# Three of the second scan's input products through ScalarE and TensorE, and all first weight parts at its first pair

## What is computed

```python
def step(h, inp):
    dt_t, B_t, C_t, x_t = inp
    dA = jnp.exp(dt_t[..., None] * A)
    h = dA * h + (dt_t * x_t)[..., None] * B_t[:, None, :]
    y = jnp.einsum('bdn,bn->bd', h, C_t)
    return (h, y)
...
for e in range(E):
    h = jax.nn.gelu(xf @ w1[e] + b1[e], approximate=False)
    y = h @ w2[e] + b2[e]
    out = out + combine[:, e:e + 1] * y
```

## Time and profile before

| | us |
|---|---|
| median of 3 runs | 208.72 |
| lowest and highest | 206.53, 208.76 |
| the profiled execution's time | 208.26 |
| its span, first to last instruction | 206.5 |
| TensorE busy in the span | 183.0 (89%) |
| weight loads | 151.8 (73%) |
| VectorE, ScalarE, GpSimd busy | 130.9, 122.5, 105.3 |

### The profile page before, as it was taken

How to read it: one execution, slowest core, us unless ns; L and a number is a source line. 1 busy time by engine, 2 the same in 40 slices (tenths; PEclk the granted TensorE clock), 3 DMA queues, 4 the chain that set the end, 5 groups by cost and what they waited for, 6 DMA issues and landing times. The chain is left out here.

```text
span 206.5 us, 3725 instructions
## 1 busy us (share of the span) xinstructions
PE 183.0 (89%) x1202; PEld 151.8 (73%) x1202; DVE 130.9 (63%) x312; ACT 122.5 (59%) x281; POOL 105.3 (51%) x140
## 2 busy tenths in 40 slices
PE   6899868996797389799998999999998999999993
PEld 5677744652262134478997989899998999999992
DVE  2575999999999869951373836562357573334333
ACT  2707998999543564424567646776555555455540
POOL 5510044779787795692555435544375344444400
PEclk9999999999999769999999999999999999999999
DMA  5950299997560000000000000000000000000000
GB/s 154 327 176 0 71 363 349 326 317 212 184 227 0 0 0 0 0 0 3 0 2 0 3 2 0 3 0 0 3 0 5 0 2 0 3 27 3 0 0 25
DMA packets 7233, 14.38 MB, mean 70 GB/s; under 512 B 512, under 2 KB 3112, under 8 KB 6960
## 3 DMA queue, kind: packets, MB, share of 16 engines
q1 hardware_dynamic: 7216, 14.17, 21.3%
HBM read 13.88 MB, written 0.29 MB: 69 GB/s over the span
## 5 line engine op out<-in xcount | busy, mean ns | idle before, releaser
L345 POOL TENSOR_TENSOR hc<-hs,cb 128x1024 f32<-128x1024 f32 x16 | 37.6, 2355 | 25.0 <-DMA cb<-c_rows 13.0
L905 DVE SCALAR_TENSOR_TENSOR acc<-dbx_ps,comb,acc 128x128 f32<-128x128 f32 x96 | 29.0, 345 | 33.4 <-PE dbx_ps L1184 33.0
L1156 PE MATMUL bc_ps<-x_hi,w_hi 128*128 128x256 f32 x128 | 42.3, 330 | 0.8 <-DVE dbx_ps L761 0.8
L612 ACT ACTIVATE hid<-bc_ps,par 128x256 f32<-128x256 f32 x64 | 26.8, 471 | 25.3 <-PE bc_ps L1158 25.1
L359 POOL TENSOR_TENSOR w_lo<-w1b,w_hi 128x256 fp32r<-128x256 f32 x32 | 23.5, 736 | 27.4 <-ACT w_hi L604 27.1
L771 DVE TENSOR_TENSOR_SCAN hs<-da,dbx_ps 128x1024 f32<-128x1024 f32 x16 | 36.4, 2278 | 0.1
L1158 PE MATMUL bc_ps<-x_hi,w_lo 128*128 128x256 f32 x128 | 36.0, 281 | 0.0
L1157 PE MATMUL bc_ps<-x_lo,w_hi 128*128 128x256 f32 x128 | 35.8, 280 | 0.0
L1184 PE MATMUL dbx_ps<-w2b,hid 128*128 128x128 f32 (+1 forms) x256 | 33.9, 276 | 0.8 <-DVE acc L905 0.8
L1184 PE MATMUL dbx_ps<-w2a,hid 128*128 128x128 f32 x256 | 34.1, 276 | 0.3 <-ACT hid L612 0.2
L359 POOL TENSOR_TENSOR w_lo<-w1a,w_hi 128x256 fp32r<-128x256 f32 x32 | 23.2, 732 | 21.6 <-ACT w_hi L604 21.6
(11 more groups left out here) (178 smaller groups left out, 233.7 us busy)
## 6 DMA issues: line engine op xcount, KB each, us to landing
w1a<-w_in SPq DMA_DIRECT2D x2, 1024.0 KB, 8.9
cb<-c_rows SPq DMA_DIRECT2D x2, 1024.0 KB, 6.1
w1b<-w_in SPq DMA_DIRECT2D x2, 1024.0 KB, 14.4
cb<-c_rows SPq DMA_DIRECT2D x2, 768.0 KB, 5.6
cb<-taps_in SPq DMA_DIRECT2D x1, 512.0 KB, 4.9
cb<-c_rows SPq DMA_DIRECT2D x2, 256.0 KB, 3.7
par<-packed_in SPq DMA_DIRECT2D x1, 473.0 KB, 3.8
x_cm<-x_in SPq DMA_DIRECT2D x2, 128.0 KB, 2.1
```

What stands on the lines that cost most here:

```text
L345: nc.gpsimd.tensor_tensor(hc[p][:], hs[p][:], cb[:, k].rearrange("p i (o t) -> p i o t", o=1).to_broadcast([128, PAIR, DC, T]), ALU.mult). ...
L612: ins = nc.scalar.activation(hid[p][:, c, :], h_ps[p][:, T * c:T * (c + 1)], ACT.Gelu, bias=par[:, bass.ds(u * UC + at, 1)])
L905: nc.vector.scalar_tensor_tensor(acc[k][:, t, :], o_ps[:, w // span % RING, 128 * t:128 * (t + 1)], comb[layer][b][:, t, bass.ds(u, 1)], a ...
L1156: nc.tensor.matmul(h_ps[p][:, T * c:T * (c + 1)], w1_hi[w][:, at], x_hi[b][:], start=True, stop=False)
```

## The change

Three pairs of batch 1's scan, m = 11, 13 and 15 (`TURNED`), no longer get their product from `spread_b` and `inputs`. Once, `turn` (TensorE, four transposes) brings `dtx` of batch 1 into token-major order in `f_ps`, and ScalarE copies it to `dtx_tok`. For each of the three pairs `token_products` (ScalarE) makes four 128x256 products with a column of `b_tok` as the scale of each partition, and `turned_product` (TensorE) turns them with eight transposes into the pair's `dbx` slot, after scan m-2 has released it. In the order of the engines: on ScalarE the copy and the products of pair 11 stand in `pair_in` of k=0, behind the decays of pairs 8 to 11 and ahead of `stage`; those of 13 behind the decays of 13 at k=2; those of 15 behind the decays of 15 at k=4, ahead of `expert_in`. On TensorE `turn` stands behind `spread_b` of pair 10, and the turned products in `pair_in` of k = 2, 4 and 6, the last one ahead of `lead`. All four `stage` steps stand at k=0, ahead of `weigh` of pair 8 on GpSimd. Counts of `b_ready` and `dbx_done` are reduced by `made`. Four scratch tiles (`dt_a`, `dt_e`, `dt_l`, `dt_q`) have one copy for both batches.

```diff
+TURNED = (NP + 3, NP + 5, NP + 7)
...
+        def made(m):
+
+            return m - sum(p < m for p in TURNED)
...
             plan += [("pair_in", 1, k)] + [(name, 0, 0) for name in before_states.get(k, [])]
-            if k in (0, 2):
-                plan += [("stage", k), ("stage", k + 1)]
+            if k == 0:
+                plan += [("stage", u) for u in range(STAGED)]
...
+            def token_products(m):
+
+                j = TURNED.index(m)
+                if j >= RING:
+                    act.wait_ge(s["dbx_pe"], j - RING + 1)
+                for i in range(PAIR):
+                    for t in range(TT):
+                        n = PAIR * (m % NP) + i
+                        ins = nc.scalar.activation(dbx_tok[j % RING][:, i, t, :], dtx_tok[:, t, :], ACT.Identity,
+                                                   scale=b_tok[:, m // NP, t, n:n + 1])
+                ins.then_inc(s["dbx_tok_ready"], 1)
+
             def pair_in(b, k):
 
                 for j in (range(AHEAD) if b and k == 0 else (k + AHEAD - 1,) if b else (k,)):
                     if j < NP:
                         decays(b, j, (j + NP * b) % AHEAD)
+                if (b, k) == (1, 0):
+                    act.wait_ge(s["turn_ps"], 1)
+                    nc.scalar.activation(dtx_tok, f_ps.rearrange("p (t d) -> p t d", t=TT), ACT.Copy).then_inc(s["turned"], 1)
+                    act.wait_ge(s["turned"], 1)
+                if b and k % 2 == 0 and NP + k + 3 in TURNED:
+                    token_products(NP + k + 3)
...
                 m = k + NP * b
-                dve.wait_ge(s["dbx_done"], m + (1 + RING))
+                if m in TURNED:
+                    dve.wait_ge(s["dbx_pe"], TURNED.index(m) + 1)
+                else:
+                    dve.wait_ge(s["dbx_done"], made(m) + (1 + RING))
...
                 m = k + NP * b + 1
-                if 1 < m < NB * NP:
+                if 1 < m < NB * NP and m not in TURNED:
                     inputs(m // NP, m % NP, m % RING)
...
+            def turn():
+
+                pe.wait_ge(s["dtx_ready"], 1)
+                for t in range(TT):
+                    for c in range(DC):
+                        ins = nc.tensor.transpose(f_ps[:, 128 * (DC * t + c):128 * (DC * t + c + 1)], dtx[1][:, c, 128 * t:128 * (t + 1)], ident[:])
+                ins.then_inc(s["turn_ps"], 1)
+
+            def turned_product(m):
+
+                pe.wait_ge(s["dbx_tok_ready"], TURNED.index(m) + 1)
+                pe.wait_ge(s["h_done"], m - 1 + RING)
+                for t in range(TT):
+                    for c in range(DC):
+                        for i in range(PAIR):
+                            ins = nc.tensor.transpose(dbx[m % RING][:, i, c, 128 * t:128 * (t + 1)],
+                                                      dbx_tok[TURNED.index(m) % RING][:, i, t, 128 * c:128 * (c + 1)], ident[:])
+                ins.then_inc(s["dbx_pe"], 1)
...
-                if m < NB * NP:
+                if m < NB * NP and m not in TURNED:
                     spread_b(m // NP, m % NP)
+                if (b, k) == (1, 0):
+                    turn()
+                if m - 1 in TURNED:
+                    turned_product(m - 1)
```

More of the change, by code:

```diff
@@ L84 @@
 conv1_ps
-b_ready dbx_done da_done h_done hc_done y_done
+b_ready dbx_done turn_ps turned dbx_tok_ready dbx_pe da_done h_done hc_done y_done
 yz_ready o_ps var3 shift3 skip_scaled inner_done sum_done shift4 rstd3 var4 rstd4 rstd5 xn_tok xn_ps x_full x_hi_ready xsplit logit_ps z_sub z_tanh comb_ready
@@ L131, in bass_metaformer @@
         c_row = sb("c_row", [NS, NB, T])
[L132 to L135, removed]
+        dt_a = [sb("dt_a", [128, DC, T])] * NB
+        dt_e = [sb("dt_e", [128, DC, T])] * NB
+        dt_l = [sb("dt_l", [128, DC, T])] * NB
+        dt_q = [sb("dt_q", [128, DC, T])] * NB
         dt = sb("dt", [128, DC, NB, T])
@@ L140, in bass_metaformer @@
         cb = sb("cb", [128, NP, PAIR, T])
+        dtx_tok = xs_b[:].rearrange("p (t c) d -> p t (c d)", t=TT)
+        dbx_tok = [sb(f"dbx_tok_{p}", [128, PAIR, TT, DI]) for p in range(RING)]
         taps_sb = cb[:, NP - DC:NP].rearrange("p c i t -> p c (i t)")
@@ L758, in inputs @@
                 dve.wait_ge(s["h_done"], m + 1)
-                dve.wait_ge(s["b_ready"], m + 1)
+                dve.wait_ge(s["b_ready"], made(m) + 1)
                 rows = (y_ps if m == 1 else b_ps).rearrange("p (i o t) -> p i o t", i=PAIR, o=1)
@@ L1065, in spread_b @@
                 m = k + NP * b
-                pe.wait_ge(s["dbx_done"], {0: 0, 1: 0, 2: 1}.get(m, m) + RING)
+                pe.wait_ge(s["dbx_done"], {0: 0, 1: 0, 2: 1}.get(m, made(m)) + RING)
                 for i in range(PAIR):
@@ L1168, in lead_1 @@
             def lead_1(layer, b):
-                pe.wait_ge(s["dbx_done"], NB * NP + RING)
+                pe.wait_ge(s["dbx_done"], made(NB * NP) + RING)
                 hidden(0, 1, 1)
```

## The result

The changed kernel takes 210.29 us (median of 6 runs, 210.08 to 211.43) against 208.66 before (6 runs, 206.53 to 208.78): a ratio of **1.0109**, 95% interval 1.0064 to 1.0154. The profiled execution took 210.26 us with a span of 208.5. The forecast was 210.4 us. A run more than 1.5% above the fastest of its kernel is left out of the ratios, and each ratio is against runs of the kernel before made beside it, so it need not be the quotient of two medians.

A forecast was written before the change was run, and what follows sets the result against it. The prediction took a chain over ScalarE and GpSimd, not VectorE's work, to set `output` 0's start; with that 1.9 us late, 208.26 + 1.9 = 210.2 us, forecast as 210.4 us, range 206.9 to 212.9.

The forecast's parts named there:

- What bounds it: 52 to 87.5 us: a chain over ScalarE and GpSimd sets `output` 0's start; the experts take the same 116 us after.
- The first part: k=0 to k=3: copy and products delay ScalarE's high parts; weigh 8 at 63.25 instead of 58.94, `skip_norm` 2.7 us late.
- The loss that comes back: Within k=0 to k=3: weigh 10 as early as before, VectorE's 1.72 us idle used up, `xg_tok` only 0.75 late.
- The second part: k=4 and k=5: products of pair 15 ahead of `x_full` add 1.65 us, so `x_full` comes 2.4 late.
- The third part: k=6: TensorE's queue behind scan 13 takes 4.25 us, so `output` 0 starts at 89.6, 1.9 late.
- The sum: Whole kernel: 208.26 + 1.9 = 210.2 us against the profiled execution, forecast as 210.4 us, 0.8% above the median.
- Transposes: TensorE, k=6: eight overlapped transposes take 1.05 us; one after another the last product would be an estimated 2.2.
- (a): Rival: the moved weight parts pay if the first part isn't late; `output` 0 0.6 earlier, 207.7 us; chance 0.17.
- (b): Rival: VectorE's work is the bound after all, so its relief comes through; `output` 0 at 84.9, 205.5 us; chance 0.06.
- (c): Rival: TensorE's clock falls to 1.2 GHz behind scan 13, adding 2.5 us; 212.9 us; chance 0.22.

The follow-up runs named there:

- e3: Changed kernel with the four high parts ahead of the copy and the products of pair 11 on ScalarE; ratio to the kernel before 0.9982.
- e2: Changed kernel with the `stage` steps back at k=0 and k=2, so only the turned products remain; ratio to the kernel before 1.0130.
- e4: Changed kernel with the products of pair 15 behind `x_full` and `x_hi` on ScalarE; ratio to the kernel before 1.0037.
- e9: e5 with `lead` ahead of the turned product of 15 on TensorE, logits left as in e5; ratio to the kernel before 0.9881.
- e1: Kernel before with all four `stage` steps at k=0 and nothing turned; ratio to the kernel before 0.9928.
- e7: Changed kernel with `lead` ahead of the turned product of 15 on TensorE, nothing else; ratio to the kernel before 1.0076.
- e6: e5 with, on TensorE, `lead` ahead of the turned product of 15 and the logits ahead of that of 13; ratio to the kernel before 0.9989.
- e10: e5 with the logits ahead of the turned product of 13 on TensorE, `lead` left as in e5; ratio to the kernel before 0.9970.
- e5: Changed kernel with both ScalarE orders turned round: high parts before pair 11's copy and products, `x_full` and `x_hi` before pair 15's products; ratio 0.9874.
- e11: e6 with six products of no use on TensorE ahead of `to_channel`; ratio to the kernel before 0.9830.

## Why the prediction was right

- **What bounds it.** The experts moved as a whole: 118.81 us behind `output` 0 before and after.
- **The first part.** Forecast weigh 8 at 63.25, `skip_norm` 70.5, scan 11 73.2, `t_tok` 75.45; measured 63.33, 70.55, 73.27, 75.46. e3 shows that the order on ScalarE is what made it late. Four products took 1.71, 1.69 and 1.70 us, 1.65 was forecast. They cost what the decays cost, which also have a scale for each partition, and not what the plain copies cost (1.32 for four).
- **The loss that comes back.** Weigh 10 at 69.52 (69.5 forecast). `skip_norm` was 2.7 us late and `t_tok` only 0.8 (18.10 to 18.93): the idle 1.72 us ahead of `t_tok` took up the rest. e2, where two low parts are back ahead of weigh 10, has `t_tok` 1.3 late, so beside the turned products the moved parts are worth 0.45 there.
- **The second part.** `x_full` 79.66 (79.7), `logit_max` 80.92 (80.95) after 2.87 us of idle (2.9). e4 takes 1.6 us away with this order alone.
- **The third part.** `output` 0 at 89.69 (89.6), scan 14's end earlier, at 88.5. TensorE's queue had the last word: 3.42 us from the start of scan 14 to `output` 0, 2.68 before. But three terms of its 4.25 us were off, and that they cancel is luck. From start to next start the transposes took 0.82 (1.05 forecast), the gates' transposes 0.14 (0.25), and from add 13 to `output` 0 it was 1.72 (1.32), the same 1.72 as before (85.97 to 87.69). And the queue won narrowly: hc 13 was there at 87.73, 0.24 us before add 13 began. The text ahead saw this order and not that it limits what a shorter queue can win, which e9 shows.
- **The sum.** 2.0 us in the profiled spans and 1.6 between the medians, for 1.9. The profile pair shares nearly the same head (first scan at 26.08 and 26.22), which is luck. The step from the sum, 210.2, to the forecast, 210.4, takes in only half of the 0.46 us between profile and median, without a reason; with all of it the forecast would have been 210.6, also within the range.
- **Transposes.** Eight took 1.04 to 1.07 us from first start to last end at 2.4 GHz, for 1.05 forecast. One after another at the 275 ns of the Trainium skill (TensorE: Matmul & The Clock Gate, section Part 4: PE-mode transpose) they would be an estimated 2.2. In the last eight of the changed kernel a single one has a median of 273 ns in the trace, which agrees with the page; but they overlap, so the trace speaks against adding up that figure for a row of transposes.
- **Rivals.** (a) priced the moved parts without the delay at 207.7 us; e3 is that kernel and took 207.45. (b) fell with e1 and e2. (c) did not happen in the changed kernel, and the gap ahead of the last transposes, put at about 2 us, was 1.00. Its clock fell twice all the same, but elsewhere: the windows from 66 to 70 and from 77 to 80 are at 0.57 and 0.50, and behind scan 13 it is at 1.00:

```profile
66.00:70.00 4.00, 4.00 (x11) 0.57 0.02 4
77.00:80.00 3.00, 2.82 (x14) 0.50 0.00 0
85.30:89.70 4.40, 4.28 (x27) 1.00 0.00 0
```

The second fall was covered by a narrow margin: the turned product of 13 took 1.92 us and ended 0.4 us before the logits could start. The sum ahead has no term for that fall, so that it cost nothing is luck as well.

## What to carry to other kernels

Before work is taken off the fullest engine, ask which wait ends last in that stretch: here VectorE was busy 91% of the time, and 3.4 us less of its work turned into waits. Work moved to a less busy engine has a place in that engine's order, and what stands behind it there pays: 1.7 us of products ahead of `x_full` cost 1.6 us, and the same products behind it nothing. A change that loses may be a good half and a bad half, so measure each alone, and then the bad half in another place.

## What had not been expected

**The head varies, and the profile's clock doesn't show it.** The same code reaches its first scan anywhere from 24.42 to 26.78 us in the 14 profiles, more than the change itself is worth. It goes with the four-tap products of the head: from 8 to 24 us their mean is lowest, 382 ns, in the profile with the earliest first scan (e7), and highest, 529, in the one with the latest (e4). TensorE from 12 to 16 us in the kernel before, e7 and e6, by form:

```profile
L998 PE MATMUL bc_ps<-xs,w_tap 128*128 128x256 f32 x12 | 4.3, 533 | 0.1
```

```profile
L1026 PE MATMUL bc_ps<-xs,w_tap 128*128 128x256 f32 x16 | 3.7, 385 | 0.5 <-DVE xs L703 0.5
```

```profile
L1029 PE MATMUL bc_ps<-xs,w_tap 128*128 128x256 f32 x10 | 4.6, 645 | 0.1
```

Their mean goes from 385 to 645 ns with a granted clock of 1.00 in all three. The longest single ones, 794 ns in before and e6, are about twice the median of 379, as if at 1.2 GHz; that the record misses a slow clock there is an inference, and no run tested it. The 2.4 us are of the size of the spread of a kernel's runs (206.53 to 208.78 in the six of the kernel before), but only one run of each kernel has a profile, so it is not shown that the head makes that spread. Reading profiles from scan 8 on removes it from the comparison.

**Moving eight transposes by one place cost 1%.** e10 differs from e5 by that alone: 0.9970 against 0.9874, and 31.76 against 28.97 us from scan 8 to `output` 0 in the profiles, at a mean clock of 0.89 against 1.00. Their intervals just touch; e6 and e9 differ by the same move alone, and theirs do not (0.9956 to 1.0023, and 0.9840 to 0.9922). That it goes through the clock is shown for e6, which has the same order, by e11's ratio; what makes the clock fall stays open, the more so as it also fell in e9's profile, where the order round the logits is e5's.
